# A graph network's edge sums on Trainium2: gathering by units of 256 edges, read through a slot table

## The reference, cut to what matters

```python
def gat(feat, src, dst, ...):
    feat_src, feat_dst, feat_v = (feat @ W + b for W, b in ...)      # [N, 8, 64]
    e = leaky(el[src] + er[dst])                                      # [E, 8]
    a = exp(e - max_dst(e)) / sum_dst(...)                            # softmax over a node's edges
    return segment_sum(feat_v[src] * a[:, :, None], dst)              # [N, 512]

def gcn_layer(x, W, b, src, dst):
    h = x @ W
    agg = segment_sum(h[src] * (dinv[src] * dinv[dst])[:, None], dst) # [N, 512]
    return agg + h * (2 * dinv * dinv)[:, None] + b

x = x + gat(relu(layernorm(x)), ...)
h = relu(layernorm(x))
h = relu(gcn_layer(h, W1, b1, src, dst)); h = relu(gcn_layer(h, W2, b2, src, dst))
x = x + h
```

## Time and profile before

| | us |
|---|---|
| median of 3 runs | 5836.12 |
| lowest, highest | 5818.93, 5842.34 |
| the profiled execution, its own time | 5850.36 |
| its span in the trace | 5848.6 |
| before the GAT aggregation | 0 to 1285 |
| GAT aggregation | 1285 to 2627 |
| residual and first GCN product | 2627 to 2873 |
| first GCN aggregation | 2873 to 4235 |
| second GCN product | 4235 to 4436 |
| second GCN aggregation | 4436 to 5779 |
| finish | 5779 to 5849 |

### The profile page before, as it was taken

One profiled execution on the slowest core, in us unless ns is written; L12 is line 12 of the kernel. 1 busy time (PEld: TensorE's weight loads), 2 busy tenths in 40 slices (PEclk: granted clock), 3 DMA queues, 4 the chain that ended last, 5 costly groups with the idle time before them and its releaser, 6 DMA issues.

```text
span 5848.6 us, 90567 instructions
## 1 busy us (share of the span) xinstructions
PE 3892.1 (67%) x16605; PEld 2163.7 (37%) x16606; DVE 3168.6 (54%) x5474; ACT 1752.4 (30%) x4252; POOL 2818.2 (48%) x3021
## 2 busy tenths in 40 slices
PE   3854069627777677668776676766797676677663
PEld 2743069615555555543322222222242222222221
DVE  6742059986666666668544444444453444444446
ACT  0210000014334333433333333333333333333332
POOL 0036620036666666655455555555424555555552
PEclk8976579859999999999888888888899888888987
DMA  4120011126666666655555555555414555555556
GB/s 139 50 80 15 5 31 50 47 86 171 174 172 173 174 172 176 173 159 173 155 159 158 156 158 154 155 156 156 141 66 132 155 156 156 153 152 152 149 151 206
DMA packets 312088, 788.69 MB, mean 135 GB/s; under 512 B 82060, under 2 KB 100378, under 8 KB 310988
## 3 DMA queue, kind: packets, MB, share of 16 engines
q0 software_dynamic: 205760, 647.72, 39.5%
q1 hardware_dynamic: 106284, 140.51, 7.3%
HBM read 716.04 MB, written 71.96 MB: 135 GB/s over the span
## 4 chain that ended last, share of the span: by engine, by line
PE 40%; issue 28%; SPq 11%; DVE 11%; DMA 4%; POOL 2%; DVEq 1%; ACT 1%; another core or an unknown queue 1%; POOLq 0%; ACTq 0%
PE mm L1436 11%; PE tr L1436 7%; SPq L974 6%; PE mm L1367 3%; PE tr L1367 3%; PE mm L1318 3%; DMA rows_w<-v_tab,row_idx 3%; PE mm L1433 3%; PE sm L1433 3%; POOL rows_w L1124 2%; PE hist_ps L1433 2%; SPq L968 2%; SPq L980 2%; PE tr L1433 2%; DVE big L738 2%
## 5 line engine op out<-in xcount | busy, mean ns | idle before, releaser
L1137 POOL DMA_INDIRECT rows_w<-h_tab,row_idx x1564 | 1477.7, 945 | 1216.6 <-SPq L980 771.2
L1436 PE MATMUL mm<-rows_w,eler_hots 128*128 x1664 | 1029.2, 738 | 700.8 <-issue 312.3
L1227 ACT ACTIVATE eler_hots<-eler_hots,ones 128x256 f32<-128x256 f32 x1272 | 646.0, 508 | 2348.2 <-PE mm L1436 961.6
L738 DVE TENSOR_TENSOR big<-big,mm 128x512 f32 x832 | 572.1, 688 | 1126.9 <-PE mm L1436 915.1
L1124 POOL DMA_INDIRECT rows_w<-v_tab,row_idx x880 | 833.7, 947 | 476.3 <-issue 260.6
L1436 PE MATMUL tr<-rows_w,eler_hots 128*128 x1664 | 923.7, 674 | 141.6 <-issue 69.8
L1221 ACT ACTIVATE eler_hots<-iota,ndrel 128x128 f32<-128x128 f32 x2544 | 881.6, 393 | 155.1
L738 DVE TENSOR_TENSOR big<-big,tr 128x512 f32 x832 | 572.0, 687 | 461.9 <-PE tr L1436 282.1
L1436 PEld LDWEIGHTS mm<-rows_w,eler_hots 128*128 128x128 f32 x1664 | 330.3, 222 | 1321.8 <-issue 1320.4
L1436 PEld LDWEIGHTS tr<-rows_w,eler_hots 128*128 128x128 f32 x1664 | 353.5, 222 | 713.2 <-issue 711.6
L1433 PE MATMUL mm<-rows_w,eler_hots 128*128 128x260 f32 x1176 | 406.0, 429 | 251.7 <-issue 135.7
(11 more groups left out here) (234 smaller groups left out, 3951.4 us busy)
## 6 DMA issues: line engine op xcount, KB each, us to landing
h_tab<-rows_w SPq DMA_DIRECT2D x98, 256.0 KB, 2.0
rows_w<-h_tab,row_idx POOLq DMA_INDIRECT x1564
rows_w<-low_tab SPq DMA_DIRECT2D x137, 128.0 KB
rows_w<-v_tab,row_idx POOLq DMA_INDIRECT x880
v_tab<-rows_w SPq DMA_DIRECT2D x49, 256.0 KB
x_tab<-big SPq DMA_DIRECT2D x49, 256.0 KB, 2.8
big<-x SPq DMA_DIRECT2D x6, 2048.0 KB, 20.0
rows_w<-x SPq DMA_DIRECT2D x48, 256.0 KB, 2.8
```

Of the source, the lines that this page charges most:

```text
L738: dve.tensor_tensor(big[:, ds(o, D)], big[:, ds(o, D)], sum_ps[bank][:, :], ALU.add).then_inc(a["acc_added"], 1)
L1137: pool.indirect_dma_start(rows[:, u, :], None, tab, bass.IndirectOffsetOnAxis(ap=row_idx[:, b, s.j % IDX:s.j % IDX + 1], axis=0)).then_inc ...
L1227: act.activation(onehot[:, s.j % 2, :, :], dist[:, :, :], ACT.Relu, bias=ones[:, 0:1], scale=-1.0).then_inc(a["onehot_set"], 1)
L1436: last = pe.matmul(sum_ps[bank][:, :], hots[0], flat_rows[:, ds(slot[0][bank], D)], start=True, stop=True)
```

## The change

All three aggregations are now gathered by units of 256 edges (`UNITS` = 391), two DMAs of 128 rows each, and every unit once. One `gather` and one `relay` serve all three.

- **GAT.** POOL issues 782 gathers in place of 880, into the same 8 slots (`RING[2]` = 4 units). SP runs the relay here too. It frees a unit when DVE has multiplied it (`msg_set`), one unit behind (`freed` = 1). DVE reads the slot of a step from a table and writes the products into one of three separate buffers in `edge` (`MSGS` = 3), which PE reads. DVE's copy of the weights is gone; ACT copies them into the same buffer, one small activation a step. DVE loads eight addresses, eight slots and four checked counts every 8 steps, and waits for landed rows once for two steps.
- **GCN.** The ring has 8 units, which is 16 slots, in `edge`, with rows 2048 bytes apart in place of 2080. SP's relay passes once for a unit, two units behind (`freed` = 2): its semaphore work and its register loads are halved for the same edges. PE's loop loads four counts and eight slots for 8 steps, and waits once for two steps for the 0/1 matrix and the rows. DVE loads eight addresses at a time.
- **Indices.** SP loads 24 at a time in all stages; POOL's index copy is gone. The preparation makes the tables for GAT too and no longer gathers GAT's source indices.
- **x1.** 20 tiles are loaded early in place of 24: 8 after the first GCN relay and 12 before the second, none inside a relay. The other 29 are loaded in `finish`.

The constants, and where the products and the GCN ring lie:

```diff
+UNITS = J // 2
+RING = {2: 4, 1: 8}
-EARLY_X1 = 2 * J * H // D // XL * XL
-IDX = 16
-FREED = 2
+EARLY_X1 = 20
+IDX = 24
+PER_IDX = IDX // 2
+OFFS = 8
+MSGS = 3
...
+        msgs = edge[:, SP * 2 * H:SP * 2 * H + MSGS * 2 * AW].rearrange("p (m c n) -> p m c n", m=MSGS, n=AW)
+        gcn_ring = edge[:, 0:2 * RING[1] * D].rearrange("p (s n) -> p s n", n=D)
+        early_x1 = edge[:, 2 * RING[1] * D:2 * RING[1] * D + 8 * D].rearrange("p (s n) -> p s n", n=D)
```

DVE in a GAT step:

```diff
-                        dve.wait_ge(a["rows_in"][u], (w - u) * 8 + 32)
-                        dve.tensor_tensor(view, view, weights.unsqueeze(3).to_broadcast([P, 2, H, F]),
-                                          ALU.mult).then_inc(a["msg_set"], 1)
-                        dve.tensor_copy(rows_w[:, 2 * u:2 * u + 2, D:AW], weights).then_inc(a["msg_set"], 1)
+                        if s.j % 2 == 0:
+                            dve.wait_ge(a["rows_ready"], need[0][s.j % OFFS // 2])
+                        got = flat_rows[:, ds(slot[0][s.j % OFFS], 2 * AW)].rearrange("p (c n) -> p c n", c=2)
+                        dve.tensor_tensor(msgs[:, s.j % MSGS, :, 0:D].rearrange("p c (h f) -> p c h f", f=F),
+                                          got[:, :, 0:D].rearrange("p c (h f) -> p c h f", f=F),
+                                          weights.unsqueeze(3).to_broadcast([P, 2, H, F]), ALU.mult).then_inc(a["msg_set"], 1)
```

SP, the relay for all three, and the early loads of x1:

```diff
+            def relay(a, done):
+
+                units, freed, free = a["units"], a["freed"], [None]
+
+                def step(s):
+                    g, u = s.k, s.j % units
+                    sp.wait_ge(a["rows_in"][u], (g - u) * (32 // units) + (32 + a["rows_before"][u]))
+                    sp.sem_inc(a["rows_ready"], 1)
+                    if s.j % PER_IDX == 0 and (s.inner or g + PER_IDX < UNITS):
+                        load_idx((s.turn * 2 + (s.j // PER_IDX + 1)) * IDX, (s.j // PER_IDX + 1) % 2)
+                    if s.j % 4 == 0:
...
+                    if s.past(freed):
+                        sp.wait_ge(done, free[0][s.j % 4])
+                        sp.sem_inc(a["slot_free"], 1)
+                pipelined(sp, UNITS, 2 * PER_IDX, 0, step)
...
+            relay(agg[0], agg[0]["msg_set"])
...
+            relay(agg[1], agg[1]["step_sum"])
+            for t in range(8):
+                sp.dma_start(x1_early(t), x1_tab[t * P:(t + 1) * P, :]).then_inc(x1_early_in, 16)
...
+            for t in range(8, EARLY_X1):
+                sp.dma_start(x1_early(t), x1_tab[t * P:(t + 1) * P, :]).then_inc(x1_early_in, 16)
+            relay(agg[2], agg[2]["step_sum"])
```

POOL, one gather for all three:

```diff
+            def gather(tab, a, ring):
 
                 def step(s):
+                    g, u, b = s.k, s.j % a["units"], s.j // PER_IDX
+                    if s.past(a["units"]):
+                        wait_alone("pool", pool, a["slot_free"], g - a["units"] + 1)
+                    if s.j % PER_IDX == 0:
+                        wait_alone("pool", pool, idx_in[b], s.turn * 16 + (16 + a["idx_before"][b]))
+                    for i in range(2):
+                        n = s.j % PER_IDX * 2 + i
                         pool.indirect_dma_start(
+                            ring[:, 2 * u + i, :], None, tab,
                             bass.IndirectOffsetOnAxis(ap=row_idx[:, b, n:n + 1], axis=0)).then_inc(a["rows_in"][u], 16)
```

PE in a GCN step (eight steps to a turn of the loop), and ACT's small copy in a GAT step:

```diff
+                    if s.j == 0:
...
+                    if s.j % 2 == 0:
+                        pe.wait_ge(a["onehot_set"], s.turn * (OFFS // 2) + (s.j // 2 + 1))
+                        pe.wait_ge(a["rows_ready"], need[0][s.j // 2])
+                    if s.past(BANKS):
+                        pe.wait_ge(a["acc_added"], w - BANKS + 1)
+                    pe.matmul(sum_ps[bank][:, :], onehot[:, s.j // 2 % 2, s.j % 2, :], edge[:, ds(slot[0][s.j], D)],
+                              start=True, stop=True).then_inc(a["step_sum"], 1)
...
+                    if per == 1:
+                        act.activation(msgs[:, s.j % MSGS, :, D:AW], w_step[:, ds(n, 1), :].rearrange("p w (c h) -> p (w c) h", c=2),
+                                       ACT.Copy).then_inc(w_col_set, 1)
```

More of the change, by code:

```diff
@@ L44 @@
 GAT, GCN = Cut(2), Cut(1)
-GPAD = -(-GCN.groups // 16) * 16
+UNITS = J // 2
+RING = {2: 4, 1: 8}
 GE = GAT.edges
@@ L92, in pipelined @@
         body(Step(k, k % unroll, count, False, k // unroll))
[L93 to L96, removed]
+    if hi > lo:
+        with eng.Fori(0, (hi - lo) // unroll) as i:
+            for j in range(unroll):
+                body(Step(i * unroll + (lo + j), j, count, True, i + lo // unroll))
+    for k in range(max(lo, hi), count + lag):
         body(Step(k, k % unroll, count, False, k // unroll))
@@ L174, in build @@
         row_idx = sb("row_idx", [P, 2, IDX], I32)
-        need_row = ndrel[0][0:1, 0:GCN.steps].bitcast(I32)
-        ends_row = src_step[0:1, 0:GCN.groups]
-        slot_row = src_flat[0:1, 0:GCN.steps]
+        slot_row = [src_flat[0:1, 0:GAT.steps], src_flat[0:1, 0:GCN.steps]]
+        need_row = [src_flat[0:1, GAT.steps:GAT.steps + GAT.steps // 2],
+                    ndrel[0][0:1, 0:GCN.steps // 2].bitcast(I32)]
         edgecols_i = sb("edgecols_i", [P, 2], I32)
@@ L739, in aggregate @@
-                pipelined(dve, c.steps, 2 * WB if weighted else 2 * BANKS, LAG, step)
+                            dve.wait_ge(a["acc_added"], 2 * w)
+                        o = offs[0][s.j % OFFS]
+                        for half, bank_ps in enumerate((sum_ps[bank], half_ps[bank])):
+                            part = big[:, ds(o + half * (AW // 2), AW // 2)]
+                            dve.tensor_tensor(part, part, bank_ps[:, 0:AW // 2], ALU.add).then_inc(a["acc_added"], 1)
+                pipelined(dve, SP, 2 * WB, LAG, step)
@@ L1142, in _ @@
             pool.wait_ge(dve_prep, marks["tables"])
             all_kept(pool, v_kept)
-            gather(v_tab, agg[0])
+            gather(v_tab, agg[0], rows)
             def seed(m, s, lag):
@@ L1408, in aggregate @@
+            def aggregate(a):
                 need, slot = [None], [None]
                 def step(s):
-                    w, u, bank = s.k, s.j % c.slots, s.j % banks
-                    if not weighted and s.j % BANKS == 0:
+                    w, bank = s.k, s.j % BANKS
+                    if s.j == 0:
                         _, need[0] = nc.values_load_multi_w_load_instructions(
-                            need_row[:, ds(w, BANKS)], engines=(mybir.EngineType.PE,), min_val=1, max_val=c.groups)
+                            need_row[1][:, ds(s.turn * (OFFS // 2), OFFS // 2)], engines=(mybir.EngineType.PE,),
+                            min_val=1, max_val=UNITS)
@@ L1415, in step @@
                         _, slot[0] = nc.values_load_multi_w_load_instructions(
-                            slot_row[:, ds(w, BANKS)], engines=(mybir.EngineType.PE,), min_val=0, max_val=(SLOTS - 1) * AW,
-                            skip_runtime_bounds_check_because="masked when the table is made")
-                    if weighted:
-                        pe.wait_ge(a["onehot_set"], w + 1)
-                        pe.wait_ge(a["msg_set"], 2 * w + 2)
-                        hots = [onehot[:, s.j % 2, n, :] for n in range(2)]
-                    else:
-                        pe.wait_ge(a["onehot_set"], s.turn * (c.slots // 2) + (s.j // 2 + 1))
-                        pe.wait_ge(a["rows_ready"], need[0][bank])
-                        hots = [onehot[:, s.j // 2 % 2, s.j % 2, :]]
@@ L1437, in step @@
-                    last.then_inc(a["step_sum"], 1)
-                pipelined(pe, c.steps, 4 * PAIRS if weighted else 8, 0, step)
+                            slot_row[1][:, ds(w, OFFS)], engines=(mybir.EngineType.PE,), min_val=0,
+                            max_val=(2 * RING[1] - 1) * D, skip_runtime_bounds_check_because="masked when the table is made")
+                    if s.j % 2 == 0:
+                        pe.wait_ge(a["onehot_set"], s.turn * (OFFS // 2) + (s.j // 2 + 1))
+                        pe.wait_ge(a["rows_ready"], need[0][s.j // 2])
```

276 lines of the change are left out of this document (135 added, 141 removed).

## The result

The changed kernel takes **5596 us** (four runs, 5576 to 5617) against 5829 us for the kernel before (four runs): a ratio of 0.960, with an interval from 0.958 to 0.963. It is faster, as forecast, but by 233 us, where 860 were forecast; 4976 us and the range from 4800 to 5330 us were both missed. The profiled execution took 5592.92 us, its span is 5591.2.

What follows compares the result with a forecast made beforehand. No engine was full: GAT's ring was too short, GCN's POOL waited for SP; afterwards POOL would bind GCN. From 5850.4 - 232 - 327 - 308 + 5 = 4988 us, less 12: 4976 us, range 4800 to 5330, chance 0.65.

Steps and rivals of the forecast that it cites:

- POOL's 978 us and the floors: GCN: 782 gathers at 1.25 us make POOL the bound at 978 us; 989 us a stage if nothing is lost.
- the last of the GCN part: GCN: unexplained standstills of SP and PE add 45 us to 989 us, giving 1035 us a stage.
- GAT's 1110 us: GAT: 391 units at 2.8 us, 1095 us, plus 15 us for beginning and end; 232 us gained from 1342.
- The way round of 6.6 to 9.0 us: GAT's ring: gather, landing, DVE's multiplication and SP's relay for three units, 2.2 to 3.0 us each; POOL needs 2.5 us.
- DVE's busy time: GAT, a sign that the forecast is right: DVE is busy for near 890 us.
- Rival A: SP's and PE's stops persist with any relay: GCN stages 1184 us, GAT 1290 us, whole 5454 us; chance 0.15.
- B: GAT's relay eats GAT's gain: way round 10.5 us, 3.5 us a unit, GAT 1369, whole 5235 us; chance 0.14.
- C: GAT: SP's stops fall inside the circle of POOL, SP and DVE, making the whole slower, 6016 us; chance 0.02.
- D: DMA queues' share rises to about 0.75 and 0.72, slower landings showing in GAT first; part of B, no separate chance.
- The rest: Outside the aggregations' gains: x1 loads, preparation and strided tables together add 5 us (-5 to +20).
- The PE clock above 0.9: GCN, a sign that the forecast is right: PE's granted clock is above 0.9.
- The register loads: GAT: DVE's three loads cost 0.34 us to twice that each; at the skill's 200 ns a register, some 110 us more.

## Why the prediction was wrong, step by step

- **POOL's 978 us and the floors** were right; 982 to 984 us is what GCN takes between first and last gather where nothing stops, with the ring of 8 units and no pauses. Nearly all of the miss of 620 us lies in three stages: 229 and 208 us in GCN, 182 in GAT.
- **The step that failed** is the last of the GCN part: "The lower end of what is lost is 0, the upper is half of the 389 us of waits. I take 45 us, nearer to 0, since the slack is doubled". Lost were 1264 - 989 = 275 and 254 us, above even the upper end of 195. I had seen the 1.4 us checks and took them for chance events that slack absorbs. They come with the very thing that the change makes denser: POOL's trains. With twice the slack the longest train of GCN 1 grew from 10 to 26 gathers and the long instructions from 310 to 720, and with a ring of 4 units there was none. The upper end had to be the whole of what the stage then lost over POOL's floor.
- **GAT's 1110 us** is 1086 where nothing stops and 1292 with stops. The way round of 6.6 to 9.0 us for three units was reckoned from undisturbed rows. GAT before had no relay and not one long instruction, only late wake-ups (105 us on ACT); with the relay it has 186, 151 of them on SP, and POOL waits 323 us for SP. DVE's busy time is 822 us, not 890: its loads are not counted there.
- **Rival A** named the right mechanism and had 0.15. Its GAT (1290) was met to 2 us, by luck in part, since it is 1110 + 180 and the runs show 1086 + 206; its GCN (1184) was not met: by keeping "half of its 389 us" it made the same mistake in size. What I put against it, "half as many SP instructions and twice the slack", is what fell: the loads were halved (98 for 196), POOL's waits for SP went from 389 to 286 us only. B has GAT at 1369 us, 77 too long, and its cause, a ring too short by itself, does not hold: without stops the same ring gives 1086 us. C fell. D fell too: with stops the DMA share is 0.56 to 0.59, and without them it reaches 0.67 and 0.73 and the stages are shorter.
- **The rest** was forecast at +5 and came to -10 us (preparation -6, between the layers +3, `between` -6, `finish` -1). The PE clock above 0.9 that I named as a sign was 0.85 with stops and 0.99 without.
- **The register loads.** Eight values take DVE 597 ns at the median (L735) where four took 344, and PE 592: neither the 200 ns a register of the Trainium skill (Runtime: NRT & Kernel Launch, instruction fetch mechanics), which it gives for registers loaded from HBM, while the tables here lie in SBUF, nor a fixed price. The Trainium skill's other figure, a floor of about 600 ns (DMA: Bandwidth & Descriptors, latency and other measured facts), is undercut by the 344 ns. Neither was what decided.

## What to carry to other kernels

Where a cheap sequencer instruction shows a maximum of forty times its median, find out what it coincides with before it is costed: compare its maximum across stages with different traffic, or run a stage with half of the suspected traffic. A wait whose cause grows with the speed that one is about to gain is not slack to be absorbed; its upper bound is all that the stage now lacks to its floor. Take a second profile on another occasion before building on one: here it could have moved the base from 5836 to 4630 us.

## What the runs showed of the hardware

With stops, while POOL issues 128-row indirect gathers 1.25 us apart in trains of 5 and more and SP runs its relay, instructions on SP, PE, DVE and ACT that take 0.02 to 0.15 us often take about 0.7 us, and wake-ups come late; POOL's gathers are not slowed (median 957 ns in both conditions). The long instructions go with the number of gathers close together, not with their bytes (64 or 512 columns alike). They are next to none where the trains are cut to pairs (1.64 us a gather on average) and with a ring of 4 units, and there are none in GAT without a relay. Late wake-ups reach further: into the old GAT (105 us on ACT) and into the preparation. There, between 392 and 798 us, SP issued 26 of its small broadcasts, while POOL gathered; without stops it issued 137 in 353 us. Each waits until DVE has used an older one, so the row shows DVE's late wake-ups (344 us, above) and not a slow issue by SP:

```profile
392.40 406.21 SPq L984 DMA_DIRECT2D rows_w<-low_tab  x26
```

```profile
389.35 353.31 SPq L984 DMA_DIRECT2D rows_w<-low_tab  x137
```

The Trainium skill (DMA: Bandwidth & Descriptors, latency and other measured facts) gives it as a best guess, for two of the DMA engines being slower than the rest, that fetching descriptors from the rings of DMAs issued by GpSimd contends for ports. A cause in descriptors would fit a cost by gathers and not by bytes, but no run here shows it, nor why the stops are absent on some occasions, with the same kernel, the same 957 ns and 208 GB/s in place of 164.
